# VectorE copies each tile's second expert matrix to fixed buffers, so that TensorE's program has no register operations

## The reference

```python
h = _layernorm(x) * (1 + cb) + sb                       # 4096 tokens of 128
score = relu(h @ rw1 + rb1) @ rw2 + rb2                 # 8 experts
_, topi = jax.lax.top_k(score, 2)
gate = softmax(where(chosen, score, -inf))
for e in range(8):
    y = relu(h @ W1[e] + b1[e]) @ W2[e] + b2[e]         # 128 -> 512 -> 128
    out = out + gate[:, e:e+1] * y
x = x + gb * out
```

## Time and profile before

| | |
|---|---|
| median of 3 runs | 504.75 us (501.91 to 505.66) |
| the profiled execution | 502.97 us, its span 501.2 us |
| mean granted clock of PE | 0.975 |
| PE busy | 434.7 us (87%), x5267 |
| DVE busy | 365.3 us (73%), x1040 |
| ACT busy | 343.5 us (69%), x1513 |
| POOL busy | 337.9 us (67%), x490 |
| chain that ended last | PE 40%, ACT 22%, DVE 16%, issue 14%, POOL 3% |

### The profile page before, as it was taken

One profiled execution on the slowest core, in us unless ns is written; L12 is line 12 of the kernel. 1 busy time (PEld: TensorE's weight loads), 2 busy tenths in 40 slices (PEclk: granted clock), 3 DMA queues, 4 the chain that ended last, 5 costly groups with the idle time before them and its releaser, 6 DMA issues.

```text
span 501.2 us, 15780 instructions
## 1 busy us (share of the span) xinstructions
PE 434.7 (87%) x5267; PEld 341.1 (68%) x5267; DVE 365.3 (73%) x1040; ACT 343.5 (69%) x1513; POOL 337.9 (67%) x490
## 2 busy tenths in 40 slices
PE   6898888988888888888889996979888989898985
PEld 5565666666666666666654443978888888887985
DVE  6767999999999999999956755545666434334776
ACT  3676999999999999999966552533544556446750
POOL 6985855554678677886743888666667666666560
PEclk9999999999999999999989998789999899999999
DMA  8461000000000130030060122133332222218436
GB/s 222 119 184 48 13 12 12 13 12 14 13 13 13 18 114 12 12 93 14 9 195 7 48 66 83 54 101 91 105 89 76 73 79 72 74 54 255 146 97 184
DMA packets 61514, 36.48 MB, mean 73 GB/s; under 512 B 25806, under 2 KB 57334, under 8 KB 61306
## 3 DMA queue, kind: packets, MB, share of 16 engines
q1 hardware_dynamic: 54682, 25.24, 19.6%
q0 software_dynamic: 4352, 9.45, 5.6%
q10 hardware_dynamic: 2400, 0.79, 0.6%
HBM read 20.56 MB, written 14.88 MB: 71 GB/s over the span
## 4 chain that ended last, share of the span: by engine, by line
PE 40%; ACT 22%; DVE 16%; issue 14%; POOL 3%; DMA 1%; another core or an unknown queue 1%; DVEq 0%; SPq 0%; ACTq 0%; POOLq 0%
ACT pr L1034 22%; PE pAm L2022 13%; DVE nmax L1101 8%; PE pSpm L2030 7%; PE pScm L2030 7%; PE pAm L1506 4%; DVE oT L947 2%; PE pm L767 1%; PE pV L761 1%; POOL y_scr L1689 1%; PE pScm L1521 1%; PE pQ L754 1%; PE pSpm L1513 1%; DVE stat L1358 1%; POOL hn L351 1%
## 5 line engine op out<-in xcount | busy, mean ns | idle before, releaser
L1034 ACT ACTIVATE pr<-pS,nmax 128x136 f32<-128x136 f32 x512 | 185.0, 380 | 13.5 <-DVE nmax L1101 13.3
L1771 ACT ACTIVATE act<-pAm,w1t 128x128 f32<-128x128 f32 x288 | 80.5, 380 | 83.5 <-remote 64.3
L1034 ACT ACTIVATION_READ_ACCUMULATOR pr<-pS,nmax 128x1 f32 x512 | 108.7, 212 | 0.0
L1689 POOL DMA_INDIRECT y_scr<-ys,si x72 | 75.2, 1045 | 37.2 <-issue 16.2
L1063 PE MATMUL pS<-kT,qbd 64*128 64x136 f32 x1024 | 93.8, 302 | 1.5 <-ACT pr L1034 1.2
L1101 DVE TENSOR_REDUCE nmax<-pS 128x4 f32<-128x544 f32 x128 | 87.6, 684 | 2.1 <-PE pS L1067 1.4
L1109 DVE STREAM_TRANSPOSE prT<-pr 128x640 f32<-128x640 f32 x96 | 81.1, 845 | 8.7 <-ACT pr L1034 0.2
L2022 PE MATMUL pAm<-hgT,w1t 128*128 128x128 f32 x576 | 80.8, 285 | 5.6 <-DVE w1t L1880 2.7
L1654 POOL DMA_INDIRECT xs<-h_all,pos_i x64 | 64.7, 1011 | 26.3 <-issue 10.6
L2022 PEld LDWEIGHTS pAm<-hgT,w1t 128*128 128x128 f32 x576 | 74.0, 201 | 7.7 <-issue 3.9
L1063 PEld LDWEIGHTS pS<-kT,qbd 64*128 64x128 f32 x1024 | 68.3, 186 | 14.6 <-ACT pr L1034 1.1
(11 more groups left out here) (293 smaller groups left out, 682.2 us busy)
## 6 DMA issues: line engine op xcount, KB each, us to landing
hg<-xs SPq DMA_DIRECT2D x72, 72.0 KB
vbd<-v_scr SPq DMA_DIRECT2D x132, 16.0 KB, 1.8
v_scr<-h_all SPq DMA_DIRECT2D x8, 256.0 KB, 2.4
h_all<-y_scr SPq DMA_DIRECT2D x8, 256.0 KB
x_all<-in_L_attn_x SPq DMA_DIRECT2D x3, 512.0 KB, 6.4
w_all<-in_L_ffn_W SPq DMA_DIRECT2D x2, 768.0 KB, 5.1
w_all<-in_L_ffn_W SPq DMA_DIRECT2D x3, 512.0 KB, 5.5
y_scr<-ys,si POOLq DMA_INDIRECT x72
```

The costliest lines, as they stand in the source:

```text
L1034: e.activation(pr[:, n, to:to + SPAN], scored(j, gi)[:, lo:lo + SPAN], ACT.Exp, bias=nmax[:, k:k + 1], scale=-1.0, accum_out=rs[u][:, k:k ...
L1689: e.indirect_dma_start(out=y_scr, out_offset=bass.IndirectOffsetOnAxis(ap=si[:, j:j + 1].bitcast(U32), axis=0), in_=ys[j % R // 2][:, j % ...
L1771: e.activation(ac(u)[:, k, :], pU[u % W][:, k, :], ACT.Relu, bias=w1t[u // 2 % 4][:, u % 2, FF + D + k:FF + D + k + 1]).then_inc(a_up.sem, 1)
```

## The change

`down` no longer reads `w2_all` by a register. DVE copies the second matrix, 512 numbers per partition, to one of 8 fixed buffers `w2t` right after the first matrix, 5 tiles ahead. Five of the buffers are new; three are memory whose earlier use is over: `rw1_sb` (the router's first matrix) and the two `hn`. The semaphore `v_w` goes up by 2 per tile instead of 1: `up` waits for the first of the two, `down` for the second (only while `known` is false; later `up(j + 3)`, which stands ahead of `down(j)`, has waited for more). PE's register loads, its waits for the lists of experts, and the register operations are gone.

```diff
+            w2t = [sm(f"w2t{u}", [P, FC * D]) for u in range(HGS - 3)]
+            w2t += [rw1_sb[:, :]] + [t[:, :, :].rearrange("p n d -> p (n d)") for t in hn]
...
-            v_w = Count(sem("m_v_w"), 1, R)
+            v_w = Count(sem("m_v_w"), 2, R)
...
                     e.tensor_copy(w1t[u // 2 % 4][:, u % 2, :], w1_all[:, bass.ds(x_, 1), :].rearrange("p a f -> p (a f)")).then_inc(v_w.sem, 1)
+                    e.tensor_copy(w2t[u % HGS][:, :], w2_all[:, bass.ds(x_ * FF, FF)]).then_inc(v_w.sem, 1)
...
                 def up(i, u, known=False):
-                    v_w.wait(e, i, u)
+                    v_w.wait(e, i, u, 1)
...
-                def down(i, u, x_, known=False):
-                    if u % 2 == 0 and not known:
-                        v_y.wait(e, i, u // 2, back=2)
+                def down(i, u, known=False):
+                    if not known:
+                        v_w.wait(e, i, u, 2)
+                        if u % 2 == 0:
+                            v_y.wait(e, i, u // 2, back=2)
                     a_up.wait(e, i, u)
                     for k in range(FC):
-                        mm = e.matmul(pY[u // 2 % 2][:, u % 2, 0:D], ac(u)[:, k, :], w2_all[:, bass.ds(x_ * FF + k * D, D)], start=k == 0, stop=k == FC - 1)
+                        mm = e.matmul(pY[u // 2 % 2][:, u % 2, 0:D], ac(u)[:, k, :], w2t[u % HGS][:, k * D:(k + 1) * D], start=k == 0, stop=k == FC - 1)
...
-                    if j in LISTS[2:-1]:
-                        e.wait_ge(v_fin, LISTS.index(j) + 1)
-                    if j % EG == 0:
-                        mine.update(zip(range(j, j + EG), experts(mybir.EngineType.PE, j)))
```

More of the change, by code:

```diff
@@ L2004, in route_tensor @@
                     group_of_router(e, g)
-                mine = {}
                 def rows(i, u, known=False):
@@ L2065, in turn @@
                         up(*at(i, u, UP_BY), known=j >= EVEN)
-                    down(i, u, mine[j], known=j >= EVEN and left >= UP_BY)
+                    down(i, u, known=j >= EVEN and left >= UP_BY)
                 tiles(e, NF, R, ROWS_BY + 1, turn, head=1, last=LOOPS)
```

## The result

The changed kernel takes **507.99 us** (median of 19 runs, 504.15 to 510.50). The kernel before, run beside it, takes 503.71 us (19 runs, 501.91 to 507.78). The ratio is **1.0077, 95% interval 1.0060 to 1.0094**: slower by some 4 us, where 490 was forecast. The profiled execution of the changed kernel is its fastest run (504.15, span 502.4), so its trace shows only about 1 us of these 4. The same kernel on two other occasions gave 1.0056 (1.0033 to 1.0080) and 1.0035 (1.0012 to 1.0057).

What follows compares the result with a forecast made beforehand. PE was taken to bound the expert loop through gaps at `down`, with POOL next. From 502.97 us: + 1.3 - 16.4 + 2.0 + 0 = - 13.1, so 489.9, stated as 490; range 482 to 500.

Steps and rivals of the forecast that it cites:

- PE's register work goes: PE in the expert loop: 24 pairs of tiles would save 0.90 us each, 22 us by PE alone; lower end nothing.
- the break: PE's `down` of even tiles coming in pieces, put down to "issue": 4.75 us a pair of tiles instead of 3.85.
- The lateness goes away with the break: ACT and DVE hear of PE's finished products 1.6 to 2.7 us late; assumed to end once `down` is whole.
- POOL next in line: POOL's indirect DMAs from 325.0 to 449.6 would set the pace, 0.97 + 0.30 us each, limiting the gain to 16.4 us.
- The start: Three new DVE copies ahead of the first `hgT`, for which PE's first `up` waits: + 1.3 us (1.2 to 1.5).
- DVE's copies, 0.42 us: Each of DVE's 72 added copies was taken as 0.42 us, between 0.39 and 0.49.
- stretch two: POOL's 24 DMAs to 386.8, forecast 32.3 us; DVE with 19 turns of 0.42 more 32.4, just fitting or up to 2 us.
- POOL stretched, + 2 us: New DVE copies delay POOL's DMAs in the expert loop: + 2 us taken, ends 0 and 20 us.
- The end: PE idles some 7 us before tile 64's rows, as SP waits for POOL; slower clock and smaller gains together 0.
- The second: Rival: the break is not the register work, PE stays at 4.75 us a pair; 505 us, chance 0.11.

Runs made afterwards that it cites:

- plain scatters: Kernel before with POOL's 72 scatters as plain instead of indirect DMAs, output wrong: 474.98 us, ratio 0.9491; on another chip 472.74 us, ratio 0.9869.
- the 500-us chip: The one of the four chips used for the experiments on which the unchanged kernel before takes 500.4 to 500.6 us.
- 480-us chips: The three of the four chips used for the experiments on which the unchanged kernel before takes 479.5 to 480.2 us.
- the experiment that took it back: Changed kernel with the second-matrix copies of tiles 0 to 4 moved behind the first two hgT: 481.89 us, ratio 1.0041 to the kernel before.

## Why the prediction was wrong, point by point

**The step that failed: "PE's register work goes", a gain of 22 us (16.4 as far as POOL follows).** Taken away alone the register work was worth 0.6 and 1.5 us (0.11% of 500, 0.32% of 480). The two rows on which the step stood show gaps on the line that holds the register operations; that is a place, not a cause. The counter-evidence was in the text, among the rivals: `down` of odd tiles has as many register operations and is whole. When the register operations went, the break stood at other lines and the period stayed: 4.67 us a pair for 4.75. What showed in its place are POOL's indirect DMAs: with plain scatters the 500-us chip takes 474.98 us for 500.59, and TensorE has no gap.

**"The lateness goes away with the break"** took the late increments for a consequence of the break at `down`. They come and go with the indirect DMAs, whatever stands in TensorE's stream: in all eight traces of the six kernels with indirect scatters on such chips a pair takes 4.5 to 4.8 us from 352 to 430 (555 to 586 records in 78 us). The earlier trace rows held the sign: a relu 1.6 us behind the end of its `up`, on an idle ACT, and a wait that the trace puts down to "remote". Whether lateness makes the break is open, as said above.

**POOL next in line, back to back at 0.97 + 0.30; 3.85 us a pair; a relu within 0.2 us.** All of this exists, at 3.78 us and 0.10 us, but as the kernel before on 480-us chips, with its register operations. The forecast of 490 priced what goes with indirect DMAs on such a chip, not what the change gives.

**The start, + 1.3 us:** 1.6 in the two profiles (2.78 to 4.35 from `rows` to `up`), 1.7 on 480-us chips. The copies there are longer than the 0.42 us charged: the three new ones take 0.60, 0.75 and 0.41 us in the profile after. On the path it is less, by the experiment that took it back.

**DVE's copies, 0.42 us:** median 0.41 to 0.42 in the profile after. The check of stretch two counted 19 turns; the trace has 15 more instructions there, for 4.5 us. **POOL stretched, + 2 us:** on 480-us chips 0.03 us a DMA, 3.8 in 136; sign and size were right there, and this is what plain scatters take away. In the two profiles of the measurement it does not show.

**The end, 0:** no stall moved to SP's wait for tile 64, since POOL was not faster. Instead the copies beside its combining fill DVE (14.3 of 15.2 us), and from the start of scatter 47 to that of the last one it takes 1.7 us longer (447.47 to 488.51, before 448.01 to 487.39).

**The rivals.** The second, the break is not the register work, 505 us with a chance of 0.11, is what happened: the period is nearly unchanged, and the time 4 us up. That its + 1.3 and + 2 make 3.3 of these 4 is partly luck: in the two profiles of the measurement the first `up` starts at the same time (313.88 and 313.90), and POOL's indirect DMAs are no longer than before. This rival deserved most of the weight.

## What to carry to other kernels

A gap in front of an instruction says where an engine waited, not why: before a step is booked as the price of what stands on that line, look for the same thing elsewhere without the gap, and for consumers that start late although they are idle. When several engines hear late of finished work, look for what else began when the lateness began; here the time of the first indirect DMA pointed at it. Compare kernels on one chip only. And where GpSimd sets the pace, copies that are added to VectorE can be paid for by GpSimd's DMAs even if VectorE has room.

## What the runs showed of the hardware that I had not expected

On one chip, and where the change was measured, indirect DMAs from POOL go together with semaphore increments that come late, TensorE's above all (2.6 us in the median, most of them 1 to 4), from the first such DMA to the last; on three other chips the same kernel shows 0.01 us. The kernel before needs 20 us more there. Plain DMAs from the same queue, of the same bytes, don't do it. **Open** is how an indirect DMA does this, by which road TensorE loses its time, why only some chips have it, and whether the recording of the profile has a part in it, since there three in four of the semaphore records are missing as well (407 for 1808) for the same stretch.
